# A four-layer token network on one core: x loaded in three parts, part of the last sum moved, two engines' code without loops

## The reference

```python
x = x + attn_a(ln(x), wq, wk, wv)                  # one head, rotary embedding, full softmax
x = x + ffn(ln(x), W1, b1, W2, b2, Wr, br)         # 8 experts, top-1 routing
x = x + attn_b(ln(x), w_q, w_k, w_v, w_o)          # 16 heads of 64, causal
x = x + ffn(ln(x), W1, b1, W2, b2, Wr, br)         # the same experts again

def ffn(x, ...):
    logits = x @ Wr + br
    idx    = argmax(logits);  gate = softmax(logits)[idx]
    h      = gelu(x @ W1[idx] + b1[idx])           # 128 -> 512
    return gate * (h @ W2[idx] + b2[idx])          # 512 -> 128
```

## Time and profile before

| what | value |
|---|---|
| runs of before | 862.47, 862.25, 859.58 us, median 862.25 |
| the profiled execution | 863.25 us, of which span 861.4 |
| PE busy | 809.8 us (94%) |
| DVE, ACT, POOL busy | 623.0 (72%), 566.6 (66%), 439.4 us (51%) |
| mean granted TensorE clock | 0.981 |
| DMA traffic | 40.04 MB, mean 46 GB/s |

### The profile page before, as it was taken

The page is one execution under the profiler, slowest core; times in us unless marked ns, Lnnn a source line. Parts: engine busy times, 40 slices in busy tenths (PEclk is TensorE's granted clock), DMA queues, the critical chain, the costliest instruction groups (busy, mean ns, idle before and its releaser), DMA issues.

```text
span 861.4 us, 24248 instructions
## 1 busy us (share of the span) xinstructions
PE 809.8 (94%) x6857; PEld 699.1 (81%) x6860; DVE 623.0 (72%) x2698; ACT 566.6 (66%) x2041; POOL 439.4 (51%) x771
## 2 busy tenths in 40 slices
PE   7999879999899999989999999999999999789992
PEld 4888748999788888878888888888778888489992
DVE  4789856666577777867777777887767776566665
ACT  2567636666577777766777777777767777256661
POOL 3343654677444544444544444544884544237772
PEclk9999989999899999999999999999999999999997
DMA  9930012313200000000000000000020000003135
GB/s 311 334 118 1 17 57 80 113 51 96 68 2 2 1 2 2 2 2 0 0 0 0 0 1 2 2 2 2 27 96 1 0 2 2 1 26 117 52 99 164
DMA packets 25930, 40.04 MB, mean 46 GB/s; under 512 B 4657, under 2 KB 17585, under 8 KB 24817
## 3 DMA queue, kind: packets, MB, share of 16 engines
q1 hardware_dynamic: 20848, 28.76, 10.3%
q0 software_dynamic: 4992, 10.27, 3.6%
HBM read 20.58 MB, written 18.43 MB: 45 GB/s over the span
## 4 chain that ended last, share of the span: by engine, by line
PE 73%; DVE 8%; POOL 7%; issue 7%; DMA 3%; ACT 1%; DVEq 1%; SPq 1%; POOLq 0%; ACTq 0%
PE PS L1166 11%; PE PS L1178 10%; PE PS L1157 10%; PE PS L1121 9%; PE PS L1130 9%; PE PS L1209 6%; PE PS L1003 5%; PE PS L1005 5%; PE PS L1004 5%; POOL xs_dram L324 3%; PE PS L1113 1%; DMA X<-in_x 1%; POOL w1b L357 1%; POOL pb L384 1%; POOL pb L382 1%
## 5 line engine op out<-in xcount | busy, mean ns | idle before, releaser
L382 POOL TENSOR_SCALAR pb<-pb,rib 128x128 f32<-128x128 f32 x256 | 95.7, 374 | 254.2 <-DVE rib L876 253.5
L867 DVE CUSTOM_DVE_ANT_0 PS<-PS,CST 128x128 f32<-128x128 f32 (+1 forms) x512 | 169.1, 381 | 66.5 <-PE PS L1178 63.4
L881 DVE COPY pT<-PS 128x384 f32<-128x384 f32 x256 | 139.8, 554 | 33.7 <-PE PS L1157 33.6
L523 ACT ACTIVATE pb<-PS,nbb 128x128 f32<-128x128 f32 x256 | 95.1, 371 | 102.2 <-DVE nbb L867 95.0
L497 ACT ACTIVATE yT<-PS,w1b 128x128 f32<-128x128 f32 x368 | 105.3, 369 | 63.4 <-PE PS L1121 63.4
L384 POOL TENSOR_SCALAR pb<-pb,rib 128x256 f32<-128x256 f32 x256 | 123.0, 481 | 0.0
L1157 PE MATMUL PS<-CST,pb 128*128 128x128 f32 x768 | 118.2, 280 | 4.3 <-POOL pb L384 3.5
L525 ACT ACTIVATE pb<-PS,nbb 128x256 f32<-128x256 f32 x256 | 121.4, 474 | 0.0
L340 POOL DMA_INDIRECT yt_dram<-XY x92 | 93.1, 1012 | 32.5 <-issue 20.0
L1157 PEld LDWEIGHTS PS<-CST,pb 128*128 128x128 f32 x768 | 86.4, 142 | 27.9 <-issue 15.6
L1166 PE MATMUL PS<-pT,vb 128*64 128x256 f32 (+1 forms) x1024 | 104.0, 340 | 1.9 <-DVE pT L881 1.6
(11 more groups left out here) (135 smaller groups left out, 1700.2 us busy)
## 6 DMA issues: line engine op xcount, KB each, us to landing
xs_dram<-XY SPq DMA_DIRECT2D x4, 1483.5 KB, 13.7
XY<-xs_dram SPq DMA_DIRECT2D x4, 1225.5 KB, 5.7
W1S<-in_W SPq DMA_DIRECT2D x1, 2048.0 KB, 20.3
W2S<-in_W SPq DMA_DIRECT2D x4, 512.0 KB, 7.7
out_dram<-X SPq DMA_DIRECT2D x8, 256.0 KB, 4.1
yt_dram<-XY POOLq DMA_INDIRECT x92, 2.4
XY<-xs_dram SPq DMA_DIRECT2D x4, 258.0 KB, 2.6
xs_dram<-TOK,POS POOLq DMA_INDIRECT x64, 2.3
```

Source lines behind the costliest of these rows:

```text
L867: last = nc.vector.tensor_tensor_reduce(ps, ps, CST[:, m:m + c1 - c0], -SCALE_B, HIGHEST, ALU.add, ALU.min, nbb[:, hh % 4, c0 // P:c0 // P ...
L881: nc.vector.tensor_copy(pT[:, hh % 4, :], PS[:, bank, 0:3 * P]).then_inc(b_pT, 1)
```

## The change

- SP loads tiles 0 to 3 of x first of all, before `CST` and `IDS`. Tiles 4 to 7 are a DMA of their own between `ROPE` and `WVA`; tiles 8 to 31 come where 4 to 31 came. DVE waits for the second part in step 2 and for the third in step 4 of attention a. The two casts from `CST` go behind DVE's step 0, and POOL waits for `half` alone.
- On DVE and ACT all steps of attention b are written out; PE and POOL keep their loops.
- Quarter `q` of the last sum's first group (4 tiles) is added in DVE's expert steps 47 to 50, behind the bias of tiles 42 to 45; SP stores these four parts before it waits for `returned[3]`.
- Of the second group's four gathers SP issues two and ACT, on its own DMA queue, two; of its four stores SP issues two and ACT two.

The diff, cut to its core:

```diff
@@ -259,15 +259,24 @@
         @block.sync
         def _(sp):
             xv = x.rearrange("b (t p) d -> p (b t) d", p=P)
+            ov = out.rearrange("b (t p) d -> p (b t) d", p=P)
+
+            def store(q0, q1):
+                for q in range(q0, q1):
+                    sp.wait_ge(x_done, q + 1)
+                    sp.dma_start(ov[:, 4 * q:4 * q + 4, :], X[:, 4 * q:4 * q + 4, :]).then_inc(s_out, 16)
+
+
+            sp.dma_start(X[:, 0:4, :], xv[:, 0:4, :]).then_inc(s_x0, 16)
             sp.dma_start(CST[:, :], cst).then_inc(s_cst, 16)
             sp.dma_start(IDS[:, :], ids).then_inc(s_ids, 16)
-            sp.dma_start(X[:, 0:4, :], xv[:, 0:4, :]).then_inc(s_x0, 16)
             sp.dma_start(WQK[:, :, :], wqk_a).then_inc(s_wa, 16)
             sp.dma_start(ROPE[:, :, :], rope).then_inc(s_wa, 16)
+            sp.dma_start(X[:, 4:8, :], xv[:, 4:8, :]).then_inc(s_x1, 16)
             sp.dma_start(WVA[:, :], wv_a).then_inc(s_wa, 16)
             sp.dma_start(WRS[:, :], Wr).then_inc(s_wr, 16)
             sp.dma_start(BRS[:, :], br.rearrange("(a e) -> a e", a=1).to_broadcast([P, E])).then_inc(s_wr, 16)
-            sp.dma_start(X[:, 4:NT, :], xv[:, 4:NT, :]).then_inc(s_x1, 16)
+            sp.dma_start(X[:, 8:NT, :], xv[:, 8:NT, :]).then_inc(s_x2, 16)
             sp.wait_ge(s_zero, 3)
             for k in range(4):
                 sp.dma_start(xs_dram[k].rearrange("(p j) d -> p j d", p=P), XY[:, 0:NJ, :]).then_inc(s_xs0, 16)
@@ -290,19 +299,18 @@
                     sp.dma_start(XY[:, g * NJ + j0:g * NJ + j1, :], xsv[:, j0:j1, :]).then_inc(xs_in[k][c], 16)
                 if k % 2 == 1:
                     for kk in (k - 1, k):
+                        if kk == 3:
+                            store(0, 4)
                         sp.wait_ge(returned[kk], 16 * (NJ - LENT if kk == 1 else NJ))
                         if kk == 1:
                             sp.wait_ge(lent_returned, 16 * LENT)
                         ytv = yt_dram[kk][0:NONE, :].rearrange("(t p) d -> p t d", p=P)
                         t0 = GT * (kk % GROUPS)
-                        for q in range(4) if kk == 3 else (0,):
+                        for q in range(2) if kk == 3 else (0,):
                             a, b = (4 * q, 4 * q + 4) if kk == 3 else (0, GT)
                             sp.dma_start(TOK[:, t0 + a:t0 + b, 0:D], ytv[:, a:b, :]).then_inc(
                                 last_gathered[q] if kk == 3 else gathered[kk], 16)
-            ov = out.rearrange("b (t p) d -> p (b t) d", p=P)
-            for q in range(8):
-                sp.wait_ge(x_done, q + 1)
-                sp.dma_start(ov[:, 4 * q:4 * q + 4, :], X[:, 4 * q:4 * q + 4, :]).then_inc(s_out, 16)
+            store(4, 6)
             sp.wait_ge(s_out, 8 * 16)
 
 
...
@@ -574,24 +582,28 @@
                     weight_parts(s - (NB + 1))
             nc.scalar.copy(one_pass(WVBh[:, :]), WVB).then_inc(b_wh, 1)
             experts(0)
-            peeled(attn_b, 1, 4)
-            turns(act, attn_b, 4, ROUTE2_AT - 1)
-            attn_b(ROUTE2_AT - 1, 0)
+            peeled(attn_b, 1, ROUTE2_AT)
             attn_b(ROUTE2_AT, 1, 0, 1)
             route(2)
             attn_b(ROUTE2_AT, 1, 1, QUADS)
-            turns(act, attn_b, 12, 16)
-            peeled(attn_b, 16, 19)
+            peeled(attn_b, 12, 19)
             experts(1)
+
+            act.wait_ge(returned[3], 16 * NJ)
+            ytv = yt_dram[3][0:NONE, :].rearrange("(t p) d -> p t d", p=P)
+            for q in (2, 3):
+                nc.scalar.dma_start(TOK[:, GT + 4 * q:GT + 4 * q + 4, 0:D], ytv[:, 4 * q:4 * q + 4, :]).then_inc(
+                    last_gathered[q], 16)
+            ov = out.rearrange("b (t p) d -> p (b t) d", p=P)
+            for q in (6, 7):
+                act.wait_ge(x_done, q + 1)
+                nc.scalar.dma_start(ov[:, 4 * q:4 * q + 4, :], X[:, 4 * q:4 * q + 4, :]).then_inc(s_out, 16)
 
 
         @block.vector
         def _(dve):
             nc.vector.memset(idle[:, :], 0.0).then_inc(s_idle, 1)
-            dve.wait_ge(s_cst, 16)
-            nc.vector.tensor_copy(upperb[:, :], CST[:, C_UP:C_UP + P])
-            nc.vector.tensor_copy(onesb[:, :], CST[:, C_ONE:C_ONE + P])
-            nc.vector.memset(half[:, :], -0.5).then_inc(s_castb, 1)
+            nc.vector.memset(half[:, :], -0.5).then_inc(s_half, 1)
 
 
             def bn_stats(ln, n, tile, slot):
@@ -642,6 +654,8 @@
                     dve.wait_ge(s_x0, 16)
                 if fixed(s) and s == 2:
                     dve.wait_ge(s_x1, 16)
+                if fixed(s) and s == 4:
+                    dve.wait_ge(s_x2, 16)
                 b = s - 4
                 if has(b):
                     dve.wait_ge(a_out_ps, b + 1)
@@ -820,6 +834,9 @@
                         nc.vector.tensor_copy(w1b1[:, w, :], W1S[:, ds(e), :])
                         wait(dve, f_y, n0 if fixed(j) and j < RING else n0 + (j - (RING - 1)))
                         nc.vector.tensor_copy(w2b2[:, (u - 2) % RING, :], W2S[:, ds(e), :]).then_inc(f_w, 1)
+                    if fixed(s) and layer == 1 and 0 <= s - (NL + 1) < 4:
+
+                        quarter(s - (NL + 1))
                     j = s
                     if has(j, NL):
                         for kk in range(GROUPS):
@@ -855,6 +872,12 @@
                         in1=X[:, ds(tile + i), :], op0=ALU.mult, op1=ALU.add)
                 if s_inc is not None:
                     last.then_inc(s_inc, 1)
+
+            def quarter(q):
+
+                dve.wait_ge(gathered[2] if q < 4 else last_gathered[q - 4], 16)
+                for b in range(2):
+                    combine(4 * q + TPB * b, x_done if b == 1 else None)
 
             def attn_b(s, u, q0=0, q1=QUADS, parts=(), so_many=(0, 0, 0, 0)):
                 hb, fb, gb, v = s - 1, s - 2, s - 3, (u + 1) % 2
@@ -962,7 +985,11 @@
                     while left[0] > 0:
                         part(left)
 
-            peeled(attn_a, 0, 8)
+            attn_a(0, 0)
+            dve.wait_ge(s_cst, 16)
+            nc.vector.tensor_copy(upperb[:, :], CST[:, C_UP:C_UP + P])
+            nc.vector.tensor_copy(onesb[:, :], CST[:, C_ONE:C_ONE + P]).then_inc(s_castb, 1)
+            peeled(attn_a, 1, 8)
             turns(dve, attn_a, 8, ROUTE0_AT - 1)
             parts = route(0)
             for s in range(ROUTE0_AT - 1, NB + 5):
@@ -975,23 +1002,15 @@
             experts(0)
             dve.wait_ge(b_wh, 5)
             nc.vector.tensor_tensor(one_pass(WVBl[:, :]), WVB, WVBh[:, :], ALU.subtract).then_inc(b_wl, 1)
-            peeled(attn_b, 1, 4)
-            turns(dve, attn_b, 4, 8)
-            peeled(attn_b, 8, ROUTE2_AT)
+            peeled(attn_b, 1, ROUTE2_AT)
             parts = route(2)
 
             attn_b(ROUTE2_AT, 1, parts=parts, so_many=(6, 2, 4, 7))
             attn_b(ROUTE2_AT + 1, 0, parts=parts, so_many=(7, 3, 0, 0))
-            attn_b(ROUTE2_AT + 2, 1)
-            turns(dve, attn_b, 14, 16)
-            peeled(attn_b, 16, 19)
+            peeled(attn_b, ROUTE2_AT + 2, 19)
             experts(1)
-            dve.wait_ge(gathered[2], 16)
-            for q in range(8):
-                if q >= 4:
-                    dve.wait_ge(last_gathered[q - 4], 16)
-                for b in range(2):
-                    combine(4 * q + TPB * b, x_done if b == 1 else None)
+            for q in range(4, 8):
+                quarter(q)
 
 
         @block.tensor
@@ -1091,6 +1110,7 @@
 
             def route(k):
                 bank, c0 = ROUTE_PLACES[k]
+                pe.wait_ge(s_castb, 1)
                 pe.wait_ge(r_step, STEPS * k + HOT_STEP)
                 hot = r_hot[:, :, :].rearrange("p e t -> p (e t)")
                 mm(PS[:, bank, c0:c0 + E * GT], upperb[:, :], hot, start=True, stop=True)
@@ -1265,7 +1285,6 @@
             pe.wait_ge(s_idle, 1)
             keep_clock(20, 6)
             pe.wait_ge(s_cst, 16)
-            pe.wait_ge(s_castb, 1)
             peeled(attn_a, 0, 8)
             turns(pe, attn_a, 8, ROUTE0_AT - 1)
             for s in range(ROUTE0_AT - 1, NB + 5):
```

8 lines of the change are left out of this document (4 added, 4 removed).

## The result

The changed kernel takes **855.15 us** (median of 7 runs, 854.63 to 856.15). The kernel before, measured 7 times in all, its first three runs among them, has a median of 860.39 (857.99 to 864.05). The ratio is 0.9933, with a 95% interval of 0.9914 to 0.9952: 5.2 us less by the medians, 5.8 by the ratio, where the sum of the prediction was 7.0. The profiled execution of the changed kernel took 855.06 us, its span 853.2, against 861.4 before: 8.2 less, which is more than the medians differ by, and part of it will turn out to be chance.

A forecast was written before the change was run, and what follows sets the result against it. PE, busy 809.8 of 861.4 us, was taken to set the time nearly everywhere. Gains of 3.0 (start), 4.0 (attention b) and 0 (end) summed to 7.0 us, giving a forecast of 855.6 us, range 851.5 to 860.2.

The forecast's parts named there:

- Attention b, 4.0: Boundary of steps 5 and 6: DVE written out has no branch back, so the batch's whole excess, 4.0 us, goes; bounds 0 and 4.0.
- the stop moves: Rival: DVE's new code makes the same stop once in another step of attention b, the 4.0 stay, 859.6 us; chance 0.10.
- many stops: Rival: written-out code stops repeatedly for fetches, each stop that PE sees costing 4.0 us, up to 867.6 us; chance 0.05.
- ACT's loops, 0: Attention b: writing out ACT's loops gains nothing, as the batch with its branch back after step 7 loses only 0.02 us.
- The start, 3.0: Start: 1.45 us from DVE's step 2 beginning earlier plus 1.53 from PE keeping its clock; bounds 1.4 and 3.5.
- I expect it to keep its clock there: Start, before batch 2's transposes: with PE's idle time cut from 3.54 to 1.55 us its clock holds, gaining 1.53.
- the term for `WVA`: Start: 256 KB more ahead of `WVA` delays it 1.0 us, and the first projection 0.55 us, to 9.8.
- the start gives little: Rival: `WVA` comes later than by bytes or the clock still falls; 1.0 of the 3.0 is left, 857.6 us; chance 0.10.
- The end, 0: Behind the last matmul: early additions and stores and two gather queues gain nothing; bounds 1.0 lost and 1.7 gained.
- the rival that feared so: Rival at the end: SP is held by the fourth store, so its two gathers start 1.5 us late, 857.1 us; chance 0.05.
- part 0 comes first: Rival at the end: gathers are served in order, the first landing 2.7 us after issue; 1.5 less, 854.2 us; chance 0.10.
- the last store: End: it finds an empty queue, with 3.5 us taken from the last addition to the program's end, against 5.0 before.

The follow-up runs named there:

- two branches back: Changed kernel with DVE's steps 4 to 9 of attention b as a loop of three turns, so two branches back are taken: 904.58 us, ratio 0.9967.
- one turn per loop: Changed kernel with DVE's steps 4 to 7 of attention b in two loops of one turn each, no branch back taken: 898.81 us, ratio 0.9915.
- the first four: Changed kernel with one part undone each: old loads 901.8 us, DVE's loops back 901.35, ACT's loops back 898.33, old end 900.15.

## Why the prediction was right, and where not

The time fell in the range and 0.5 us below the forecast of 855.6; by difference, 5.2 to 5.8 us were gained of the 7.0 summed. The terms:

**Attention b, 4.0: right in place and in cause, and as a size right for the pair of profiles alone.** Put back, DVE's loop brings the stop back; two branches back bring two; loops without a taken branch bring none. So the rivals "the stop moves" and "many stops" are out: written-out code showed no such stop: DVE has no wait by issue between 250 and 590 us, and none over 1.1 us in the rest of attention b. What the term mixed up is the wait and the clock behind it. The stop costs 2.7 to 2.9 us, three times out of three in the experiments, where the clock stayed at 1.00. In the profile of before the clock fell behind it (0.95 over the batch), and that was the other 1.3. I had taken a cost that came in one execution for one that comes in each. By medians on one chip the loop is worth 3.0 (901.35 against the 898.33 with ACT's loops, which cost nothing).

**ACT's loops, 0: right.** With them in, no batch is longer. In the kernel before ACT, POOL and PE branch back beside DVE's stop too (377.5 to 378.4 us), so its trace alone could not say whose branch it was; the two experiments can. The Trainium skill, "Runtime: NRT & Kernel Launch", section "Instruction fetch mechanics", says that a taken branch to code outside what is held waits for a fetch. Had each of ACT's three branches back stopped PE as DVE's does, that would have been 12 us more. The measurements divide the cases: 317 instructions back stop DVE for 3.0 to 3.2 us, and 187 on ACT do not stop it visibly. The stop at the taken branch agrees with the rule; what each engine holds at its branch no run here shows, so its condition stays untested.

**The start, 3.0: the mechanism right, the chance in it not seen.** The profiles with the old loads and with those of the change can be laid side by side by two numbers, the start of the first projection and the start of attention a's last transposes:

| profile | first projection | last transposes | between | clock, 0 to 50 us |
|---|---|---|---|---|
| before | 9.30 | 96.77 | 87.5 | 0.97 |
| start undone | 10.24 | 97.43 | 87.2 | 0.93 |
| changed kernel, first chip | 10.21 | 95.21 | 85.0 | 0.97 |
| DVE's loops back | 9.97 | 94.93 | 85.0 | 0.97 |
| old end | 9.95 | 95.47 | 85.5 | 0.97 |
| one turn per loop | 9.75 | 95.32 | 85.6 | 0.97 |
| changed kernel, other chip | 9.21 | 94.77 | 85.6 | 0.97 |
| ACT's loops back | 9.38 | 93.21 | 83.8 | 1.00 |
| gathers on SP | 9.03 | 92.85 | 83.8 | 1.00 |
| two branches back | 10.54 | 94.40 | 83.9 | 1.00 |

Where the clock holds, 83.8 us lie between the two, 3.5 us less than before on average, whatever the moment of the projection; a clock that falls costs 1.1 to 1.7. The execution with ACT's loops back is what the prediction drew, to 0.5 us at each point: projection at 9.38 (foretold 9.8), step 2 of DVE at 13.88 (14.4), PE's idle time before the transposes 1.46 (1.55), next projections 1.99. The step that failed is "I expect it to keep its clock there": after 1.46 us of idle time it kept it in that execution and lost it in others (the kernel with `WVA` first has the same 1.46 and then 3.62 for the projections). And the term for `WVA`, 0.55 from its 250 KB a us, is itself a range: over the eight profiles with this order the first projection starts from 9.03 to 10.54, on average at the 9.8 foretold. The premise that PE is in its 20 matmuls until 8.21 us "in any case" was false: they end between 7.0 and 8.6, and an early end lengthens the wait in which the clock can fall. The mean of the eight puts the last transposes at 94.5, of the two with the old start at 97.1: 2.6 gained, between the bounds of 1.4 and 3.5, though from only two profiles on one side and with the luck of the clock in both means. The rival "the start gives little" is half true: 1.5 in the profiled execution, and the fallen clock it named, but at the first projection instead of before batch 2.

`WVA` first was no better by time. It starts everything a us sooner and finds the clock fallen in its one profile with that edit alone; with the gathers on SP as well, the clock held (last transposes at 93.0). By place it is better: over the four profiles with `WVA` ahead, two of them with a fallen clock, the last transposes start at 93.5 on average, 1.1 us before those of the eight.

**The end, 0: mis-sized by 1.4, near its upper bound of 1.7.** Three terms, counted from the last bias addition. The gathers, foretold 3.3 behind it, came after 2.99: SP's early stores hold nothing up, and the rival that feared so is out. The first part, foretold to land 3.5 after its issue because two parts are in flight, was used after 3.44: right, and "part 0 comes first" (2.7) is out. The Trainium skill says in "Queues, rings and completion order", page "DMA: Bandwidth & Descriptors", that the engines take turns between queues; the traces agree: the first part is used 3.4 to 3.7 us after its issue in the eight profiles with two queues, and 2.7 to 3.0 us after it in the six with one. From issue to the last addition's end 8.85 was foretold, and 8.45 came. But the largest miss is the last store: I took 3.5 us from the last addition to the end, and it was 2.74, nearly the gather's 2.7 that I had as the lower bound. Sum of the misses: 0.3 + 0.4 + 0.8 = 1.5. Over all profiles the old end takes 15.6 and 15.8 us from the last bias addition, the new one with two queues 14.2 on average (14.0 to 14.5): 1.5 gained.

**The experts, not in the sum:** the lead falls from 8.0 to 6.8 us between 567 us and the last bias addition, and from 7.5 at 749 us on there are 0.7 of it. I had 0.2 for the additions between the bias additions; the bias of tile 43 came 0.47 us late against its neighbours, close to the 0.55 foretold, but the last matmuls did not shift with it. The additions are not the loss: from the bias of tile 34 to that of tile 45 the kernel with the old end, which has none of them there, takes 20.8 us, the others on the three chips 20.4 to 20.8. Nor is it the clock, which fell at 748 us in this execution: the lead stood at 7.5 through that fall until 762. Whether the rest belongs to the change wasn't separated.

**The whole.** Of the 8.2 us between the two profiled spans 1.7 are the clock at the start of attention b, which the change does not touch. Without it 6.5 are left. By the experiments the parts are worth 2.6 + 2.8 + 1.5 = 6.9 us in the places where they act; less the loss of up to 1.1 behind the stop that is 5.8, beside the 5.2 to 5.8 of the runs (4.1 to 7.4 by the interval of the ratio). Medians on the chip of the first four, each against 898.33, give 3.5, 3.0 and 1.8 for the three parts, with runs of one kernel that spread over 2.5 to 4.1 us. It is the prediction's sum from other terms: less for the start and the stop, more for the end, and a loss that it lacked. That the total came out close was in part luck. The range was also summed wrongly: its named bounds, 2.2 us below the forecast, and 2.7 for a low run give 850.7, not 851.5; the result lies inside either.

No version measured is clearly faster than the changed kernel. The lowest median, 897.8 with the gathers on one queue, is 1.0 us ahead of two others on its chip (898.77 and 898.81), about what the traces show at the end, and by less than an interval in time.

## What to carry to other kernels

When a trace shows a stop and a lowered clock behind it, price them apart: the stop comes each time, the clock only in some executions, and two or three profiles of one kernel show which is which. A loop's branch back costs only where it is taken, where the trace shows the engine stop behind it (here DVE's 317 instructions, not its short loops, ACT's 187 or PE's 1260), and where others wait for that engine; only such loops are worth writing out. At the end of a kernel, put work and stores that are ready early in front of the last wait, keep transfers that are needed in order on one queue, and let the engine whose closing drain is long finish first.
